# Four input-projection groups moved out of the output projection, in an eight-core recurrent layer

## The reference

```python
xz = einsum('btd,ed->bte', x, Win);  xi, z = split(xz, 2)
lam = exp(-8 * softplus(omega) * sigmoid(xi @ Wl.T + bl))
v   = xi @ Wv.T + bv
# for each step t:
Qh = h - 2.0 * v_t * (sum(v_t * h) / sum(v_t * v_t))
h  = lam_t * Qh + (1.0 - lam_t) * xi_t
y  = (silu(z) * h) @ Wout.T
x1 = layernorm(x + y)
x_int = clip(round(x1 / scale), -127, 127)
out = layernorm(x1 + (x_int * scale) @ (ternary - 1).T + bias)
```

## Time and profile before

| | us |
|---|---|
| median of the two timed runs | 4194.7 |
| the two runs | 4171.7, 4217.7 |
| the profiled execution | 4033.4 |
| its span (core 1, the slowest; cores 3992.6 to 4031.8) | 4031.8 |
| mean granted TensorE clock, core 1 | 0.902 of full speed |

### The profile page before, as it was taken

The page is one execution under the profiler, slowest core; times in us unless marked ns, Lnnn a source line. Parts: engine busy times, 40 slices in busy tenths (PEclk is TensorE's granted clock), DMA queues, the critical chain, the costliest instruction groups (busy, mean ns, idle before and its releaser), DMA issues.

```text
span 4031.8 us, 53209 instructions; the slowest of 8 cores (3992.6 to 4031.8 us)
## 1 busy us (share of the span) xinstructions
PE 3254.8 (81%) x20764; PEld 2563.4 (64%) x20764; DVE 1306.7 (32%) x2380; ACT 563.6 (14%) x1454; POOL 220.0 (5%) x164
## 2 busy tenths in 40 slices
PE   4866668547997899887997899788987799889965
PEld 3644456325885488755885589656875488647842
DVE  1023552323243305223243306222423305221553
ACT  0001001002201112102201102111201220111211
POOL 0000000100002000010002000110002000100020
PEclk9977779778998899988998999988998899899967
DMA  4444432334632365234632465234533454245602
GB/s 139 143 175 172 172 126 80 96 100 137 200 116 89 115 207 180 79 115 141 199 110 88 128 208 168 84 131 152 199 100 103 143 190 136 84 136 176 196 15 84
DMA packets 171369, 545.28 MB, mean 135 GB/s; under 512 B 20083, under 2 KB 28660, under 8 KB 167028
## 3 DMA queue, kind: packets, MB, share of 16 engines
q1 hardware_dynamic: 163444, 516.72, 39.6%
q0 software_dynamic: 5376, 16.78, 1.4%
q10 hardware_dynamic: 2304, 8.39, 0.5%
HBM read 491.48 MB, written 50.33 MB: 134 GB/s over the span
## 4 chain that ended last, share of the span: by engine, by line
PE 60%; DMA 17%; DVE 10%; issue 5%; ACT 4%; POOL 2%; SPq 1%; DVEq 0%; ACTq 0%; POOLq 0%
PE pb L152 58%; DMA WIN<-w_in 4%; DMA WOU<-wos 2%; DMA WLV<-w_l 2%; DMA R<-w_l 1%; DVE XFM L765 1%; DMA WLV<-w_v 1%; SPq L157 1%; DMA WLV<-wls 1%; DMA WOU<-w_out 1%; DMA R<-w_v 1%; DMA Y<-w_out 1%; DMA WLV<-wvs 1%; DMA WIN<-w_ffn 1%; PE pb L709 1%
## 5 line engine op out<-in xcount | busy, mean ns | idle before, releaser
L152 PE MATMUL pb<-XI,WLV 128*128 128x256 bf16 x11520 | 1295.6, 276 | 92.8 <-DVE WLV L309 39.5
L152 PEld LDWEIGHTS pb<-XI,WLV 128*128 128x128 bf16 x11520 | 1138.2, 99 | 250.0 <-issue 104.5
L152 PE MATMUL pb<-XFM,WIN 128*128 128x256 f32 x4096 | 1012.4, 406 | 138.7 <-DMA WIN<-w_in 78.1
L152 PEld LDWEIGHTS pb<-XFM,WIN 128*128 128x128 f32 x4096 | 821.6, 204 | 302.1 <-issue 178.0
L152 PE MATMUL pb<-WOU,LAM 128*128 128x512 bf16 x1440 | 340.6, 392 | 67.1 <-DVE WOU L858 33.7
L388 DVE TENSOR_TENSOR_SCAN GC<-LAM,ZRO 128x256 f32<-128x256 f32 x128 | 88.6, 692 | 758.3 <-ACT LAM L365 745.9
L152 PEld LDWEIGHTS pb<-WOU,LAM 128*128 128x128 bf16 x1440 | 139.9, 100 | 256.6 <-issue 116.4
L260 DVE TENSOR_TENSOR XI<-pb,XI 128x256 bf16<-128x256 f32 x128 | 53.6, 423 | 507.4 <-ACT XI L257 496.5
L757 POOL TENSOR_TENSOR KK<-VB,GB 128x512 f32<-128x512 f32 x16 | 44.4, 2778 | 2663.4 <-ACT GB L733 2663.4
L152 PE MATMUL pb<-XI,Y 128*128 128x256 bf16 x768 | 120.0, 334 | 78.5 <-DVE LAM L382 39.7
L943 DVE TENSOR_TENSOR R<-pb,XTM 128x512 f32<-128x512 f32 x32 | 22.1, 690 | 445.6 <-PE pb L152 442.0
(11 more groups left out here) (167 smaller groups left out, 2198.8 us busy)
## 6 DMA issues: line engine op xcount, KB each, us to landing
WIN<-w_in SPq DMA_DIRECT2D x256, 512.0 KB, 3.7
WLV<-wls SPq DMA_DIRECT2D x224, 512.0 KB, 5.0
WLV<-wvs SPq DMA_DIRECT2D x224, 512.0 KB, 4.7
WOU<-wos SPq DMA_DIRECT2D x224, 256.0 KB, 3.1
XFM<-x_fm POOLq DMA_DIRECT2D x64, 128.0 KB, 7.6
XTM<-x_tm POOLq DMA_DIRECT2D x16, 512.0 KB, 5.4
WLV<-w_l SPq DMA_DIRECT2D x8, 1024.0 KB, 7.9
wls<-WLV SPq DMA_DIRECT2D x16, 512.0 KB, 4.5
```

The costliest lines, as they stand in the source:

```text
L152: return e.matmul(o, l, rr, start=st, stop=sp)
```

## The change

The four groups that were pumped one at a time in the first half of the output projection (after chunks 3, 7, 11 and 15 of dg = 0) are pumped before it, together with the four that already stand there. The number of groups, their order among themselves and all else stay.

```diff
@@ -820,7 +820,7 @@
         t_gfull = t_g21
         if s1n is not None:
             s1n["zgate"] = list(t_g21)
-        pump(4)
+        pump(8)
         t_state = r.do("vector", lambda e, i=fm3(GC, TT - 1, TT).squeeze(2):
                        e.tensor_copy(STATE[:, :], i),
                        waits=(t_state_pe,) + tuple(t_h), inc="dv")
@@ -894,8 +894,6 @@
                 wou_free[sl] = gtok[2 * dg + (TT // 128) - 1]
                 t_jmm = wou_free[sl]
                 womm[ic % 2] = t_jmm
-                if ic % 4 == 3 and dg == 0:
-                    pump(1)
 
         if tile == 0:
             split_done["stage"] = split_done["stage"] + (wosp[1], woout[1])
```

## The result

| | before | changed |
|---|---|---|
| median of all runs, us | 4279.7 (10 runs, 4037.6 to 4425.2) | 4432.8 (11 runs, 4075.0 to 4454.3) |
| ratio | 1 | 1.0111, 95% interval 1.0069 to 1.0153 |
| profiled execution, us | 4033.4 | 4083.9 |
| its spans, mean of the 8 cores, us | 4016.1 | 4061.4 |

The change makes the kernel 1.1% slower, some 45 us. In seven of the eleven runs of the changed kernel the cores of at least one die showed a mean granted clock near 0.78 instead of 0.90 and the run took 4432 to 4454 us, so the medians are not to be compared, and the ratio leaves such runs of both kernels out.

A forecast was written before the change was run, and what follows sets the result against it. TensorE was taken as the bound, 81% busy. 5.0 us for each of tiles 1 to 6 (30 us) plus 11 in tile 0 made 41 us, ratio 1.010: 4194.7 became 4237 us, range 4170 to 4290.

The forecast's parts named there:

- the bound: Whole kernel: TensorE busy 81% of the span; time is lost only where it stands or runs below 2.4 GHz.
- the long wait: TensorE's 8.31 us stand at the gate before the output projection; claimed to stay, gain 0 from the moved groups.
- the groups in a row: Tiles 1 to 6, before the output projection: three moved groups wait for their input weight loads, 1.5 us per tile.
- G31: Last of the next tile's 32 input groups, at the tile's end: 5.1 us lost to waiting and lower clock; upper end.
- rival B: Row before the output projection: last moved group always waits like G31; +82 us or more, about 4280; chance 0.11.
- the output projection: Tiles 1 to 6: without groups dg = 0 waits for weights as dg = 1 does; +3.5 us per tile.
- tile 0: First tile's serial output-weight load, split and store chain starts late, first split at 757.7 us, 5.3 us steps; +11 us.
- The sum: Whole kernel: 30 us for tiles 1 to 6 plus 11 for tile 0, 41 us, 1.0% more; 28 to 82.
- rival C: Faster: tile 0's chain gains 10 us, dg = 0 costs nothing; -4 us, about 4190; chance 0.08.
- Rival A: Tiles 1 to 6 hide the loads behind slower TensorE; only tile 0 pays, +11 to +20 us, about 4210; chance 0.19.
- the step from the sum to the time: Whole kernel: median of two timed runs, 4194.7 us, times 1.010 gives 4237 us.
- a clock of 13/16 of full speed: TensorE: a skill's claim for dense matmuls on three or more cores of a die; set aside, windows showed 1.00.

The follow-up runs named there:

- e3: Changed kernel with six output-weight slots instead of two in tiles 1 to 7: 66.7 us per output projection with its preceding groups in tiles 1 to 6; no ratio.
- e4: Kernel before with six output-weight slots instead of two in tiles 1 to 7: 64.9 us per output projection with its preceding groups in tiles 1 to 6; no ratio.

## Why the prediction was right and wrong

**Right: the bound and the long wait.** TensorE bounds the stretches of tiles 1 to 6, the wait at the gate stayed (6.4 to 8.4 us in the rows above), and the moved groups didn't fill it.

**Right: the groups in a row.** Forecast 1.5 us per tile; the waits in the rows are 0.84 + 0.94, and e3 against e4 leaves 1.8. The clock did not fall there (1.00 in the window above), and G23 did not pay what G31 pays in the earlier trace rows, so rival B is out. One part was costed at nothing and isn't quite: in tile 0 of core 1 TensorE waited 0.52 and 0.61 us before G21 and G23 for an evacuation by ScalarE, not for a load.

**Right: the output projection.** Forecast +3.5 us per tile by letting dg = 0 do what dg = 1 did; e3 and e4 together give 3.1. The traces can also be split directly, means over the 8 cores and tiles 1 to 6, with 4 x 3.45 us for the moved groups taken off where they stand: up to the first output matmul 2.0 us more (1.5 forecast), dg = 0 2.6 more (2.65), dg = 1 0.4 more (0.85). Sum per tile 5.0 forecast, 4.9 measured. The waits that the profile puts down to WOU grew less than I said: on core 1 from 15.2 to 24.5 us, not to 36.

**Nearly right: tile 0.** Forecast a first split 19.7 us after the start of G19 (757.7 less 737.96) and steps of 5.3 us; measured 20.2 and 5.35. From that +11 was forecast; core 1's chain shows +12.3, its stretch +10.8, and the mean of all cores' stretches is +14.8. The start was right (20.6 us later than before, 20.4 forecast). The steps were sized too small: the sixteen take 87.8 us in the mean of the cores, 5.49 each and up to 5.63 on core 3, not 5.3, and that is 3 us. I had read the step from core 1 alone. Why cores 2 and 3 are slower there wasn't tried.

**The sum** was 41 us, ratio 1.010; measured 1.0111, and 45 us between the spans. Two products in the prediction are a little off, without effect on its bounds: G31's price in every tile adds 6 x (6.1 - 1.5) = 28 us and not 25, and rival C's steps give back 4 x 2.8 = 11 us and not 10. Rival A (hidden anyway) is out where the ratio was taken; what the change costs while TensorE's clock is lower wasn't measured. Rival C is out too: its condition, a chain that starts less than 10 us later, is met nowhere, the start slips by 20.6 us. With early loads the changed order is shorter in tile 0 all the same, since the steps then give back more than that.

**Wrong: the step from the sum to the time.** I multiplied the median of two timed runs by the ratio and allowed 15 us for the spread of such a median. Those two, 4171.7 and 4217.7, stood for nothing fixed: ten runs of the same kernel spread from 4037.6 to 4425.2, 388 us, with a median of 4279.7, and the changed kernel's 4432.8 lies 196 us above my 4237 and outside 4170 to 4290. The 3.4 to 4.6% between timed and profiled execution stood in the prediction and should have been read as a spread of that size, not as an offset that both kernels share: the fastest timed runs, 4037.6 and 4039.6, lie at the profiled one's 4033.4.

A lower clock that can stretch a run was in the traces. The prediction set a clock of 13/16 of full speed (0.81) aside, because no row showed it. The kernel before has such stretches on core 1, 15 us long, with TensorE busy throughout; and in the profiled execution of e3, which took 4172.7 us, core 3 spends this window at 0.81 while core 4 of the same execution has 1.00:

```profile
70.20:85.20 15.00, 15.00 (x59) 12.70 (x58) 1.70 (x4) 1.15 (x3) 0.00 (x0) 0.81 0.45 123
```

```profile
996.00:1118.00 122.00, 122.00 (x925) 100.98 (x924) 8.79 (x19) 23.33 (x53) 0.00 (x0) 0.81 0.49 158
```

```profile
996.00:1118.00 122.00, 119.51 (x1089) 105.90 (x1088) 27.89 (x60) 24.76 (x57) 0.00 (x0) 1.00 0.62 197
```

(The first is the kernel before, the second core 3 and the third core 4 of e3.) None of the runs of 4432 to 4454 us was profiled, so that this is what makes them longer is likely and not shown, and what brings a core to 0.81 stays open.

## What to carry to other kernels

Work that is inserted between steps fed by double-buffered loads isn't only filler for its own sake: it gives the loads time, and its own load comes free, as in tiles 1 to 6. Where the steps are paced by a chain of DMAs, as in tile 0, the groups' own loads stand in that chain: with early loads each group waited 5 to 6 us. Before moving such work, look at the steps next door that run without it (here dg = 1) and price the move from them. Where a queue issues load, split, store and next load in turn, put the next load ahead of the stores; that was worth some 60 us in the output projection of tile 0 and some 155 in its gates and vectors, nearly five times the 45 us that the order of the groups cost.

## What the runs showed of the hardware

I had taken the stage with 1 MB loads and stores for bound by bytes, at 173 GB/s; 282 GB/s were reached in the same stage with only the order of issue changed. And the output projection, at 200 GB/s by an estimate (1 MB per 5.2 us), needed no more bandwidth, only earlier issues: its waits went from 17.9 us on core 5 to none in the profile with four more slots. TensorE's granted clock has a third value in these traces besides 0.50 and 1.00, namely 0.81, and two cores can differ in it in the same window.
